# Binary 3x3 convolution after group norm: the padded rows of signs 32 values apart in place of 30

## What is computed

```python
def _gn(v, G=32, eps=1e-5): ...   # group norm, no scale and no shift

# _L0_conv_ref(x, M, Z, alpha, rv)
A = m * m + jnp.sum(z * z, axis=0) / 100.0
inv = lax.rsqrt(A)
w = (rv @ (z * inv))[0] + m * inv
bw = jnp.sign(w).reshape(M.shape)
ba = jnp.sign(x)
out = lax.conv_general_dilated(ba, bw, window_strides=(1, 1), padding=((1, 1), (1, 1)), ...)
return out * alpha

x = x + _L0_conv_ref(_gn(x), M, Z, alpha, rv)
```

## Time and profile before

| | |
|---|---|
| median of 3 runs | 542.02 us (541.94 to 542.55) |
| the profiled execution, its own time | 543.91 us |
| its span, from the first to the last instruction | 542.2 us |
| TensorE matmul busy | 502.3 us (93%) |
| VectorE busy | 371.9 us (69%) |
| ScalarE busy | 328.6 us (61%) |
| GpSimd busy | 23.0 us (4%) |
| mean granted TensorE clock | 0.98 of full speed |
| from and to HBM | 124 MB, 229 GB/s over the span |

### The profile page before, as it was taken

The page is one execution under the profiler, slowest core; times in us unless marked ns, Lnnn a source line. Parts: engine busy times, 40 slices in busy tenths (PEclk is TensorE's granted clock), DMA queues, the critical chain, the costliest instruction groups (busy, mean ns, idle before and its releaser), DMA issues.

```text
span 542.2 us, 8289 instructions
## 1 busy us (share of the span) xinstructions
PE 502.3 (93%) x2794; PEld 404.7 (75%) x2794; DVE 371.9 (69%) x711; ACT 328.6 (61%) x566; POOL 23.0 (4%) x70
## 2 busy tenths in 40 slices
PE   0897959899999999999999999999999999999991
PEld 0443538688888888888888888888888888888881
DVE  1122457657967967977868868769778778776646
ACT  1776766477567567666676676676666666754310
POOL 8200000000000000000000000000000000000000
PEclk9998997989999999999999999999999999999997
DMA  7999947018658558568468468468467577434226
GB/s 236 395 393 393 384 173 315 0 70 287 228 188 297 212 201 299 191 222 301 177 214 299 174 216 297 181 220 301 173 236 284 183 248 271 182 141 178 81 98 237
DMA packets 45644, 124.37 MB, mean 229 GB/s; under 512 B 3632, under 2 KB 3632, under 8 KB 45616
## 3 DMA queue, kind: packets, MB, share of 16 engines
q1 hardware_dynamic: 45616, 124.01, 63.2%
HBM read 72.62 MB, written 51.38 MB: 229 GB/s over the span
## 4 chain that ended last, share of the span: by engine, by line
PE 85%; SPq 4%; DMA 4%; DVE 3%; ACT 2%; issue 2%; DVEq 0%; ACTq 0%
PE conv_ps L339 81%; SPq L230 4%; DMA m_sb<-in_L_conv_M_dram 4%; PE conv_ps L279 1%; DVE x_sb L683 1%; PE conv_ps L292 1%; ACT whole L395 1%; DVE bn L608 1%; PE grp_ps L322 1%; PE conv_ps L282 1%; PE conv_ps L296 0%; ACT signs L444 0%; DVE whole L658 0%; PE wt_ps L312 0%; DVE low L590 0%
## 5 line engine op out<-in xcount | busy, mean ns | idle before, releaser
L339 PE MATMUL conv_ps<-signs,wts 128*128 128x448 f32 (+2 forms) x1926 | 444.7, 393 | 2.4 <-ACT signs L444 2.0
L339 PEld LDWEIGHTS conv_ps<-signs,wts 128*128 128x128 f32 x1926 | 366.4, 191 | 72.8 <-ACT signs L444 2.5
L452 ACT ACTIVATE part<-conv_ps 128x448 int32<-128x448 f32 (+2 forms) x107 | 60.0, 561 | 166.3 <-PE conv_ps L339 166.3
L658 DVE SCALAR_TENSOR_TENSOR whole<-conv_ps,part 128x448 int32<-128x448 f32 (+2 forms) x107 | 69.1, 646 | 94.7 <-PE conv_ps L339 84.1
L444 ACT ACTIVATE signs<-x_sb,shift,rstd 128x784 fp32r<-128x784 f32 x128 | 126.0, 1037 | 0.8 <-DVE shift L645 0.8
L666 DVE SCALAR_TENSOR_TENSOR low<-whole,conv_ps 128x448 f32<-128x448 int16 (+2 forms) x107 | 68.8, 643 | 3.7
L683 DVE SCALAR_TENSOR_TENSOR x_sb<-whole,alpha_sb,x_sb 128x784 f32<-128x784 int16 x64 | 65.9, 1030 | 0.7
L683 DVE SCALAR_TENSOR_TENSOR x_sb<-low,alpha_sb,x_sb 128x784 f32<-128x784 f32 x64 | 65.8, 1028 | 0.0
L627 DVE BATCH_NORM_STATS2 bn<-x_sb 128x6 f32<-128x392 f32 x116 | 59.7, 556 | 1.0 <-issue 0.7
L425 ACT ACTIVATE unread<-x_sb 128x784 bf16<-128x784 f32 x58 | 49.1, 847 | 0.0
L423 ACT ACTIVATE unread<-x_sb 128x784 bf16<-128x784 f32 x58 | 49.1, 847 | 0.0
(11 more groups left out here) (46 smaller groups left out, 149.1 us busy)
## 6 DMA issues: line engine op xcount, KB each, us to landing
x_sb<-in_x_dram SPq DMA_DIRECT2D x64, 784.0 KB, 5.7
out_dram<-x_sb SPq DMA_DIRECT2D x64, 784.0 KB, 3.9
x_sb<-in_L_conv_Z_dram SPq DMA_DIRECT2D x64, 288.0 KB, 8.0
m_sb<-in_L_conv_M_dram SPq DMA_DIRECT2D x8, 288.0 KB, 9.7
alpha_sb<-in_L_conv_alpha_dram SPq DMA_DIRECT2D x2, 0.5 KB, 2.4
rv_sb<-in_L_conv_rv_dram SPq DMA_DIRECT2D x1, 4.0 KB, 2.4
```

Of the source, the lines that this page charges most:

```text
L339: mm = pe.matmul(conv_ps[bank(b)][:, 0:columns(b)], wts[:, ch, tap], e, start=n == 0, stop=n == PRODUCTS - 1, skip_group_check=True)
L452: nc.scalar.activation(part[:, bank(b), 0:columns(b)], conv_ps[bank(b)][:, 0:columns(b)], ACT.Copy, scale=-FRACTION / PACK, bias=FRACTION ...
L658: nc.vector.scalar_tensor_tensor(out=image_tile(whole[:, t % 2], b), in0=flat_tile(conv_ps[bank(b)][:, 0:columns(b)], b), scalar=FRACTION ...
```

## The change

The constant PW, the distance between two padded rows of `signs`, becomes 32. PH stays 30.

```diff
-    PH, PW = H + 2, W + 2
+    PH, PW = H + 2, W + 4
```

## The result

The changed kernel takes 553.44 us (median of 4 runs, 552.26 to 554.01), the kernel before 542.28 us beside it. The ratio is 1.0198, 95% interval 1.0172 to 1.0224: 2% slower, 11 us, where I had forecast no change.

What follows compares the result with a forecast made beforehand. TensorE's matmuls were taken to bound the kernel. All terms were taken as 0 against the profiled 543.91 us; with the runs' median 1.9 us lower, the forecast was 542.0 us, no change, range 538 to 546.5 us.

Steps and rivals of the forecast that it cites:

- What bounds the kernel: TensorE's L339 matmuls set the time, 90 of them and some 20.65 us per triple; other engines have reserve.
- What one matmul takes: L339 start-to-start distances 215.6, 243.2, 162.8 ns; 13.2 ns a row, 1.5 to 1.7 over its columns, 4.4 per matmul.
- The third of my arguments: Step-free matmul operands of 288 values showed only 2.5 ns rest, so the extra was taken to belong to row changes.
- Does the extra depend on the row step?: L339 matmul rows: a fixed price per row change, whatever step and alignment; taken as 0, bounds -56 to +27 us.
- the form with two long skips: Three-image matmuls of 3 x 6 rows: two skips over 1,600 values; 243.2 ns against 242.0 expected, read as no skip price.
- The term 32,256 x 0: All 32,256 matmul rows of the kernel times no added cost from the new step: 0.
- The line count: 16-byte SBUF lines touched by a row's three taps: 23 in total at steps 30 and 32, so 0.
- Placement, +-0.7 us: Tile addresses: two kinds of triples differ by 0.06 us; all becoming one kind gives -0.7 or +0.7 us, taken as 0.
- ScalarE's writes: Signs of 1.036 us may each change by 0.19 us; four could show, 0.8 us either way; taken as 0.
- The memset: GpSimd's 9.10 us memset grows by 0.6 us for 720 more values, hidden by 53 us of cover; taken as 0.
- Rival 1: The matmul rows' extra goes away with aligned rows: 486 us, or 523 us for a third of it; 8 in 100.
- Rival 2: Matmul rows at a power-of-two step meet on the same piece of memory: +3.0 us, 545 us; 20 in 100.

Runs made afterwards that it cites:

- e6_flat: Kernel before the change, matmuls reading 448, 504 or 336 values in one piece in place of rows of 28, so the convolution's values differ; 517.79 us.
- e11: Kernel before the change (step 30) with all sign images 1 value further on; 543.88 us beside 543.08.
- e1_tail: Kernel before the change (step 30) with 720 unused values behind the sign images, moving later tiles 2880 bytes; 542.32 us beside 542.98, ratio 0.9994.
- e5_lead1: Changed kernel (step 32) with all sign images 1 value (4 bytes) further on; 566.79 us.
- e10_place0: Changed kernel (step 32) with every tap read from the first column, leaving out the taps' horizontal shift; 523.03 us.
- e7_wts2: Changed kernel (step 32) with the weights 2 values (8 bytes) further on and the signs where they were; 552.33 us.
- e2_step36: Kernel before the change with a step of 36 values in place of 30; 558.96 us, ratio 1.0287.

## Why the prediction was wrong

- **What bounds the kernel**: right. Nearly the whole loss lies in the matmuls of L339; the clock (1.00), TensorE's two waits and VectorE's time stayed as they were.
- **What one matmul takes**: the distances were right, the split was not. I took 4.4 ns as the matmul's own part, from a straight line through the forms of 12 and 16 rows, and gave all of a row's 13.2 ns over 11.7 to the change of row. e6_flat shows that without any change of row the straight line is nearly the same: from 336 to 448 values (203.8 - 153.7) / 4 = 12.5 ns for each 28 values, and 3.4 ns left. So about 0.9 of my 1.5 ns a row was never the row's. Against e6_flat the rows cost 12 ns in the form of 16, not 25; the rest over the columns, 17.1 ns there and 13.7 at 336, is in every matmul. The third of my arguments fails here too: the 2.5 ns that I read from the earlier trace rows for operands in one piece do not hold for these matmuls.
- **Does the extra depend on the row step? This step failed.** I took 0 from the form with two long skips, which cost "1.2 ns together more than two short ones", "about the error of the reading". By e6_flat's base, the changes of row in that form cost 243.2 - 227.1 = 16 ns in all, under 1 ns each. The new step turned out to add 0.32 ns a row; two changes dearer by that much would have shown as 0.6 ns, less than the error that I named. The form could not tell 0 from what happened. And each form mixes places at a step of 30, which I noted and then read as "a fixed price for each change of row". What the runs show in its place is a price that goes by where the rows begin: at a step of 32 it is 0.21, 0.22 and 0.23 us for the three columns of taps, against 0.21 to 0.22 before, and at 30 a shift by one value changes nothing (e11). The term 32,256 x 0 was in truth 1512 rows x 0.32 ns = 0.48 us a triple, 10 us in all.
- **The line count**: I counted 23 lines for three rows at either step, each row by itself. At a step of 30 neighbouring rows share lines: 16 rows and their gaps touch 120.25, not 16 x 23/3 = 122.7. Counted over the whole matmul, at the assumed 4 cycles a line, it comes to +0.35 us a triple and about 550 us; measured +0.48 us and 553 us. So the sum of 0 by this rule came from my way of counting. Counted whole, it would have given the sign and most of the size, but the same count missed three later forecasts, and that the page's rule is the cause is not shown.
- **Placement, +-0.7 us**: right at a step of 30 (e1_tail 0.9994; e11_step30_lead1 with one kind of triple only, 543.88 us), but no bound at 32, where a shift of the signs by one value is worth 13 us (e5_lead1). **ScalarE's writes**: 1.059 in place of 1.037 us on the mean, and TensorE's wait for them is 2.0 us as before. **The memset**: 9.70 us, nobody waited for it:

```profile
L542 POOL MEMSET signs<- x1: 9698/9698/9698, 7.4 to 7.4; 128x11520 f32 x1
```

- **Rival 1** (alignment frees the extra) was right for one place in four: e10_place0 shows 523 us if all taps could begin at a line. At a step of 32 only one column of taps does, and the two others pay more than they did in the mixture. That 523 us is also what rival 1 gave for a third of the extra is chance.
- **Rival 2** had the sign and, nearly, the place: each row of a matmul at the same place. Its mechanism got no support: for meetings with weight loads see e7_wts2, and e10_place0 is 30 us quicker with the weight loads, ScalarE and VectorE at the same step and the same places as in the changed kernel. Its price of 3 us was too low since I let only the 0.14 us over my own model be at stake. A power of two has no part in it either: 36 values are slower than 32 (e2_step36).

## What to carry to other kernels

When the rows that a matmul streams through the array (its moving operand) have a step, try the step just over the row's length first: it beat the aligned one here (529 us at 29, 542 at 30, 553 at 32). Counting the 16-byte lines that the whole operand touches, not each row by itself, gave the right order for these three and a wrong one between 31 and 32; take it as a guide to what to run. Alignment paid here only where all reads began at a line; with taps 4 bytes apart they cannot. A price drawn from a line through a few forms does not tell a cost per row from a cost per column: one run with the values in one piece does. And ask of the row that speaks for "no effect" whether it could show an effect of the size at stake.

## What was not expected of the hardware

- A matmul of float32r values in one piece, with a weight load for each, took 17.1 ns over its columns at 2.4 GHz at 448 and at 504 columns, and 13.7 ns at 336 (e6_flat). At 17.1 ns that is some 33 us of the kernel for 1926 matmuls (an estimate), and no layout of the signs tried here went below e6_flat's triple.
- A shift of the whole operand by 4 bytes is worth 13 us at a step of 32 values (553.44 to 566.79 us) and nothing at 30.
- One border value in place of two, shared between rows, made the kernel 2.6% faster with the computation unchanged; it is the best version found here that computes all that the reference does.
